# Perceiver block on one core: self-attention in sixteen written-out units with a transposed output, its end interleaved with the output projection

## Chip, cores and metric

The kernel is one program on one core of a Trainium2 chip. The metric is device time in microseconds (us) of one execution, lower is better. The profile is one execution of its own.

## What is computed

Three residual blocks on x of shape (8, 128, 512), cut from the reference:

```python
x = x + cross_attention(layernorm(x), ctx_768, mask, W_q, W_k, W_v, W_o, b_o)   # 8 heads of 64, 8 x 2048 context rows
x = x + self_attention(layernorm(x), Wq, Wkv, Wo)
x = x + ffn(layernorm(x), w_gate, w_up, w_down)                                 # ternary weights, 8-bit activations

def self_attention(h, Wq, Wkv, Wo):          # h: L=8, B=128, 512; 16 heads of 64
    q = (h @ Wq).reshape(L, B, 16, 64)
    k, v = split(h @ Wkv, 2)                 # each (L, B, 16, 64)
    score = einsum('ibnd,jbnd->ijbn', q, k) / 8
    prob = softmax(score, axis=1)            # over j: 8 rows of the same column b
    vec = einsum('ijbn,jbnd->ibnd', prob, v).reshape(L, B, 1024)
    return vec @ Wo
```

The self-attention runs along the first axis of x: each of the 128 columns attends over its own 8 rows. The kernel takes 16 columns times 8 rows as one group of 128 tokens, so there are 8 groups, and one group's scores are a 128 x 128 block of which a constant mask leaves the entries of equal column.

## The kernel before, in words

Every engine has a hand-written instruction list, and semaphores order the engines. All loads and stores are issued by SyncE (SP), in one queue. Weights and activations of most products are split in a high and a low part in a reduced float32 format, and `product` (L536) sums high x high, low x high and high x low, so a product over 512 inputs is 12 matmuls and one over 1024 inputs is 24.

The stages in order of time: query projections; cross-attention, a loop over 8 batches and their live chunks of 256 context rows (13 chunks here); the values of the self-attention for all heads, written to `v_all`; self-attention; output projection together with the transposes of the feed-forward weights; feed-forward.

**Cross-attention, where the change touches it.** `load_chunk` (L316) on SP waits until TensorE has transposed the last context chunk (`cxT_ps`) and until VectorE has turned the last mask row into a bias (`bias_done`), then issues the context load and the mask load. TensorE's `turn_context` (L604) of the next chunk runs after the first scores of the current one. On ScalarE (L989 to L991) the order is two exponentials of the current chunk, then `context_high`, which the next keys (`keys`, L617) wait for.

**Self-attention.** One step of a loop is a pair of heads, `pair(m, first)`, with m from 0 to 7; pair 0 is written out and the loop of pairs 1 to 7 is `Fori(1, PAIRS)`. A pair has two halves of four groups (512 tokens). On TensorE (L816) the order is: query projection and key projection of half 0 (`project`, 12 matmuls each), `finish_pair` of the pair before, query projection of half 1, `scores2` of half 0, key projection of half 1, `turn2` (transposes of the probabilities) for both heads of half 0, `attend2` for both heads, `scores2` of half 1. `attend2` (L800) keeps the transposed probabilities (128 columns) as weights and streams 64 columns of `v_all`, so the result has tokens on the partitions. ScalarE copies queries and one head's transposed probabilities and runs `exp2` (L1088, four exponentials with their sums for each head and half); VectorE copies keys and the other head's probabilities, takes maxima (`top2`, L1549), and in `output2` (L1561) divides by the sums while it copies the result to `o_tok`. The two engines also prepare the weights of the next pair (`weights_high` L1068, `weights_low` L1529, one buffer `wqk`), quantise one eighth of the feed-forward weights per pair (`ternary_clip`, `ternary_round`, `ternary_finish`), and split one eighth of the output weights (`output_weights_high`, `output_weights_low`). GpSimd does nothing in this stage.

**Output projection** (TensorE L837, ScalarE L1140, VectorE L1641, SP L396 to L413). After the last pair, for each of 8 tiles n: ScalarE copies the tile to `o_g`, TensorE transposes it (8 transposes), ScalarE and VectorE split it (`oT`), TensorE transposes tile n of the ternary weights (24 transposes, copied out in three parts), then runs the product of 24 matmuls, and VectorE adds it to `x_all`. `x_all` was stored in `x_mid_dram` and is read back in another token order by eight loads, one per batch, each of which writes 16 partitions (L406). They are issued after the last ternary piece has been stored and the first two have been read back. The feed-forward stage begins when all eight tiles are there (L901).

Of the kernel before, what the change touches and what calls it, by code (L numbers as in the profile page):

```python
# [5 lines left out]
ALU = mybir.AluOpType  # L6
# [8 lines left out]
P = 128  # L15
# [10 lines left out]
def bass_perceiver_block_kernel(nc, x, ctx_768, mask, xa_wq, xa_wk, xa_wv, xa_wo, xa_bo,  # L26
# [30 lines left out]
    with ExitStack() as ctx:  # L57
# [44 lines left out]
        qs = sb("qs", [P, 2, 16])  # L102

# [56 lines left out]
        o_tok = at("o_tok", 88, G, HD2)  # L160
        qT2 = at("qT2", 156, 2, 512)
        kT2 = at("kT2", 160, 2, 512)
        p2 = at("p2", 164, 2, 512)
        pT2 = at("pT2", 168, 2, 512)
        wqk_raw = at("wqk_raw", 8, 2 * DK, P)
        wqk = Split("wqk", 80, 2 * DK, P)
# [4 lines left out]
        tstage = at("tstage", 140, 2, 3 * PIECE, dt=BF16)  # L171
        o_g = at("o_g", 152, 2, HD2)
        oT = Split("oT", 160, 2, HD2)
# [4 lines left out]
        xn_f = at("xn_f", 180, 2, D)  # L178
        xq = at("xq", 76, 2, D, dt=BF16)
        xqT = at("xqT", 78, 2, D, dt=BF16)  # L180
# [13 lines left out]
        def sems(engine, names):  # L194
# [6 lines left out]
         absw_in0, absw_in1, xg_in, wqk_in, wo2_in, traw_in, tern_out, tst_in0, tst_in1, y_out, consts, const_step) = sems(  # L201
            None, "x_in0 x_in1 x_in wq_in wk_in wv_in wo_in bo_in mask_in code_out code_in cx_in mrow_in x_mid_out wv2_in "
            "absw_in0 absw_in1 xg_in wqk_in wo2_in traw_in tern_out tst_in0 tst_in1 y_out consts const_step")
        absw_in, tst_in = [absw_in0, absw_in1], [tst_in0, tst_in1]
        (xnT_ps, q_ps, qT_ps, cxT_ps, kT_ps, s_ps, v_ps, pT_ps, pv_ps, onT_ps, lnT_ps, xo_ps, v2_ps, mean_ps, qk_ps,
         s2_ps, pT2_ps, o2_ps, oT_ps, y2_ps, wT_ps, xqT_ps, g_ps, u_ps, hqT_ps, y_ps) = sems(
            "pe", "xnT_ps q_ps qT_ps cxT_ps kT_ps s_ps v_ps pT_ps pv_ps onT_ps lnT_ps xo_ps v2_ps mean_ps qk_ps "
            "s2_ps pT2_ps o2_ps oT_ps y2_ps wT_ps xqT_ps g_ps u_ps hqT_ps y_ps")
        (wq_hi, wk_hi, wo_hi, xnT_hi, q_done, qT_hi, cxT_hi, kT_hi, v_done, p_done, alpha_done, pT_act, onT_hi, lnT_hi, xo_done,
         wv2_hi, lnTg_done, v2_act, wqk_hi, qT2_done, p2_done, pT2_act, tern_rounded, wo2_hi, og_done, oT_hi, wT_act,  # L210
         xq_done, xqT_done, sg_done, h_round, hq_done, hqT_done, y_scaled) = sems(
            "act", "wq_hi wk_hi wo_hi xnT_hi q_done qT_hi cxT_hi kT_hi v_done p_done alpha_done pT_act onT_hi lnT_hi xo_done "
            "wv2_hi lnTg_done v2_act wqk_hi qT2_done p2_done pT2_act tern_rounded wo2_hi og_done oT_hi wT_act "
# [11 lines left out]
        (rstd_a, wv_hi, w_lo, zeroed, biased, x_mid, rstd_c, rstd_f, scales_done, down_scaled, y_done) = sems(  # L225
            "pool", "rstd_a wv_hi w_lo zeroed biased x_mid rstd_c rstd_f scales_done down_scaled y_done")
# [31 lines left out]
        def live(eng, bits, flag):  # L258

            eng.reg_alu(flag, bits, 1, ALU.bitwise_and)  # L260
            eng.reg_alu(bits, bits, 1, ALU.logical_shift_right)
            return eng.If_ne(flag, 0)

# [33 lines left out]
        def _(sp):  # L297
# [94 lines left out]
            sp.dma_start(tern_dram[PAIRS - 2], tern[:]).then_inc(tern_out, 16)  # L392
            sp.wait_ge(tern_done, START + PAIRS)
            sp.dma_start(tern_dram[PAIRS - 1], tern[:]).then_inc(tern_out, 16)

            sp.wait_ge(o2_ps, START + 4 * PAIRS)  # L396
            sp.wait_ge(tern_out, 16 * PAIRS)

            def load_ternary(piece, u, turned):
                sp.wait_ge(wT_ps, turned)  # L400
                sp.dma_start(tstage[:, u, :], tern_dram[bass.ds(piece, 1)].rearrange("a p n -> p (a n)")).then_inc(tst_in[u], 16)

            for u in range(2):
                load_ternary(u, u, START)
            sp.wait_ge(wo2_lo, START + PAIRS)
            for b in range(B):  # L406
                sp.dma_start(x_all[16 * b:16 * b + 16, :, :],
                             x_mid_dram[b].rearrange("(g q) d -> q g d", q=16)).then_inc(xg_in, 16)
            with sp.Fori(1, G // 2) as t:
                pieces = [sp.snap(2 * t + u) for u in range(2)]  # L410
                turned = sp.snap(START + 6 * t)
                for u in range(2):
                    load_ternary(pieces[u], u, turned)  # L413
# [118 lines left out]
        def _(pe):  # L532
# [237 lines left out]
            def project(m, half, which):  # L770

                if half == 0 and which == 0:
                    pe.wait_ge(wqk_lo, START + m + 1)
# [967 lines left out]
```

## Time and profile before

| | us |
|---|---|
| median of 3 runs | 836.67 (836.04 to 839.28) |
| the profiled execution's own time | 834.46 |
| its span, first to last instruction | 832.5 |

Busy, as a share of the span: TensorE matmul 84% (697.4 us), its weight loads 66%, VectorE 53%, ScalarE 46%, GpSimd 9%. The mean granted TensorE clock is 0.926 of full speed. Read busy time by stage, since each stage has another limit, and read a matmul's own duration with care: matmuls overlap in the pipeline, so the distance from one to the next says more.

### The profile page before, as it was taken

The page shows a single profiled execution, that of the slowest core. Times are in us where ns is not written, and L with a number is a line of the kernel's source. Part 1 is how long each engine was busy: PE and PEld are TensorE (multiplying, and loading weights), DVE is VectorE, ACT ScalarE, POOL GpSimd, SP SyncE. Part 2 cuts the span into 40 slices and gives each one's busy share as a digit, 9 for nine tenths or more (in the row PEclk, how much of TensorE's full clock was granted, in tenths as well). Part 3 has the DMA queues.
Part 4 walks back from the last instruction along what each step waited for, and adds up shares of the span by engine and source line. Part 5 has one row for each costly group of instructions (what it writes and reads, how often), then busy time and mean ns, then how long its engine had stood idle before and what let it go on. Part 6 is the DMA issues. An engine that isn't in the chain of part 4 may idle for free.

```text
span 832.5 us, 15880 instructions
## 1 busy us (share of the span) xinstructions
PE 697.4 (84%) x4310; PEld 551.9 (66%) x4338; DVE 440.3 (53%) x964; ACT 380.0 (46%) x888; POOL 75.5 (9%) x120
## 2 busy tenths in 40 slices
PE   3978579889696969699598999999997499989994
PEld 2767468778585858587386777777776388635452
DVE  6644335534544445446477366665564124699960
ACT  3233324434342444344233466666554235368884
POOL 2480000100101010101100000000000000112211
PEclk9999789979898889799699899999996799999998
DMA  8010000000000000032488224444435912000111
GB/s 291 0 44 0 20 20 20 20 0 20 20 20 20 20 0 20 20 94 115 159 308 289 93 80 144 141 145 138 136 122 173 156 72 79 0 1 14 25 25 38
DMA packets 40133, 64.67 MB, mean 78 GB/s; under 512 B 4138, under 2 KB 20522, under 8 KB 40114
## 3 DMA queue, kind: packets, MB, share of 16 engines
q1 hardware_dynamic: 40114, 64.45, 24.4%
q8 instruction: 8, 0.13, 0.1%
q14 instruction: 11, 0.09, 0.0%
HBM read 53.95 MB, written 10.49 MB: 77 GB/s over the span
## 4 chain that ended last, share of the span: by engine, by line
PE 64%; issue 12%; DVE 8%; ACT 6%; DMA 4%; DVEq 3%; SPq 1%; POOL 1%; ACTq 0%; POOLq 0%
PE bank L545 35%; PE bank L680 6%; PE bank L889 5%; PE bank L806 4%; PE bank L668 3%; PE bank L897 3%; ACT p L1094 3%; DMA x_all<-x_mid_dram 2%; PE bank L653 2%; PE bank L788 2%; PE bank L797 1%; DMA wq_raw<-in_L_xattn_W_q_dram 1%; DVE oT_lo L1276 1%; PE bank L784 1%; DVE amax L1552 1%
## 5 line engine op out<-in xcount | busy, mean ns | idle before, releaser
L979 ACT ACTIVATE probs<-probs,negm 128x256 f32<-128x256 f32 x104 | 52.1, 501 | 105.3 <-DVE negm L1401 105.3
L1401 DVE CUSTOM_DVE_ANT_0 probs<-bank,bias,negm_old 128x256 f32<-128x256 f32 x104 | 46.0, 480 | 60.6 <-PE bank L653 58.4
L1094 ACT ACTIVATE p<-bank,nmax 128x128 f32<-128x128 f32 x128 | 45.0, 378 | 44.4 <-DVE nmax L1554 44.4
L453 POOL TENSOR_TENSOR rstd<-var_eps,neg_half 128x1 f32 (+1 forms) x16 | 10.4, 650 | 592.9 <-DVE var_eps L1623 329.4
L889 PE MATMUL bank<-w_T,xqT 128*128 128x512 bf16 x248 | 57.3, 379 | 4.9 <-ACT xqT L1163 2.0
L653 PE MATMUL bank<-kT_hi,qT_hi 64*128 64x256 f32 x104 | 22.8, 436 | 44.7 <-issue 44.4
L680 PEld LDWEIGHTS bank<-v_sb,pT 128*128 128x128 f32 x416 | 52.3, 191 | 5.5
L680 PE MATMUL bank<-v_sb,pT 128*128 128x64 f32 x416 | 54.7, 274 | 0.0
L972 ACT COPY v_sb<-bank 128x512 f32<-128x512 f32 x28 | 15.1, 590 | 76.5 <-PE bank L680 73.5
L1276 DVE TENSOR_TENSOR kT_lo<-bank,kT_hi 128x512 fp32r<-128x512 f32 x28 | 19.4, 692 | 57.8 <-ACT kT_hi L968 57.8
L653 PEld LDWEIGHTS bank<-kT_hi,qT_hi 64*128 64x128 f32 x104 | 11.1, 210 | 54.0 <-issue 47.0
L889 PEld LDWEIGHTS bank<-w_T,xqT 128*128 128x128 bf16 x256 | 24.1, 98 | 34.2 <-DVE h_f L1670 2.5
L545 PE MATMUL bank<-cxT_hi,wk_hi 128*128 128x256 f32 x168 | 36.4, 328 | 3.2 <-ACT cxT_hi L962 2.7
L545 PE MATMUL bank<-ln_T_hi,wqk_hi 128*128 128x512 f32 x128 | 38.2, 421 | 0.0
L806 PE MATMUL bank<-v_all,pT 128*128 (+1 forms) x256 | 34.1, 288 | 2.9 <-ACT pT L1101 2.9
L1552 DVE TENSOR_REDUCE amax<-bank 128x4 f32<-128x512 f32 x32 | 22.0, 688 | 26.4 <-PE bank L788 26.4
L1524 DVE TENSOR_REDUCE asum<-absw 128x3072 f32 x8 | 26.8, 3354 | 17.2 <-DMA absw<-in_L_ffn_w_down_dram 17.2
L806 PEld LDWEIGHTS bank<-v_all,pT 128*128 128x128 f32 x256 | 32.0, 200 | 5.8 <-issue 4.5
L545 PE MATMUL bank<-ln_T_hi,wqk_lo 128*128 128x512 f32 x128 | 35.3, 398 | 0.0
L545 PE MATMUL bank<-ln_T_lo,wqk_hi 128*128 128x512 f32 x128 | 35.2, 398 | 0.0
L897 PE MATMUL bank<-wd_T,hqT 128*128 128x512 bf16 x124 | 30.3, 396 | 5.1 <-ACT hqT L1187 4.8
L668 PE MATMUL bank<-ident,probs 128*128 128x128 f32 x208 | 33.0, 284 | 0.0
(213 smaller groups left out, 1664.6 us busy)
## 6 DMA issues: line engine op xcount, KB each, us to landing
tern_dram<-tern SPq DMA_DIRECT2D x8, 768.0 KB, 3.6
tstage<-tern_dram SPq DMA_DIRECT2D x8, 768.0 KB, 5.6
cx<-in_ctx_dram SPq DMA_DIRECT2D x14, 384.0 KB, 3.0
absw<-in_L_ffn_w_gate_dram SPq DMA_DIRECT2D x8, 512.0 KB, 3.8
absw<-in_L_ffn_w_up_dram SPq DMA_DIRECT2D x8, 512.0 KB, 4.8
absw<-in_L_ffn_w_down_dram SPq DMA_DIRECT2D x8, 512.0 KB, 6.1
tern_raw<-in_L_ffn_w_gate_dram SPq DMA_DIRECT2D x8, 512.0 KB, 4.6
tern_raw<-in_L_ffn_w_up_dram SPq DMA_DIRECT2D x8, 512.0 KB, 5.8
```

The lines of the kernel that those rows point to most:

```text
L545: last = mm(to, left(k, a), right(k, b), start=(n == 0), stop=(n == 3 * nk - 1))
L653: last = mm(bank[3 + j][:, 0:CHUNK], part(qT, a)[o:o + DH, g, :], part(kT, c)[o:o + DH, g, :], start=(a == c), stop=(a == "lo"))
L668: last = tr(bank[5 + g % 2][:, at:at + P], probs[:, 2 * g + j, t * P:(t + 1) * P], ident[:])
L680: last = mm(bank[7][:, h * DH:(h + 1) * DH], pT[:, g % 2, at:at + P], v_sb[:, t, h * DH:(h + 1) * DH], start=(t == 0), stop=(t == CT - 1))
L806: last = mm(bank[6 + j][:, a * DH:(a + 1) * DH], pT2[:, j, g * P:(g + 1) * P], v_all[:, a, bass.ds(m * P + DH * j, DH)], start=True, stop= ...
L889: last = mm(bank[3 + 2 * which + c % 2][:], xqT[:, u, k * P:(k + 1) * P], w_T[:, which, k, c * 512:c * 512 + 512], start=(k == 0), stop=(k ...
L897: last = mm(bank[7][:], hqT[:, k * P:(k + 1) * P], wd_T[:, k, :], start=(k == 0), stop=(k == FK - 1))
L979: fn(probs[:, h, :], probs[:, h, :], ACT.Exp, bias=negm[:, h:h + 1], scale=-1.0, accum_out=csum[:, h:h + 1]).then_inc(p_done, 1)
L1094: last = fn(p2[:, j, g * P:(g + 1) * P], bank[2 + j][:, g * P:(g + 1) * P], ACT.Exp, bias=nmax2[:, j, g:g + 1], scale=SCALE, accum_out=sum ...
L1276: return tt(to, of, f32(hi), ALU.subtract)
L1401: nc.vector.tensor_tensor_reduce(probs[:, h, :], bank[3 + h % 2][:, 0:CHUNK], bias[:], -SCALE, negm_old[:, h:h + 1], ALU.add, ALU.min, neg ...
L1552: red(amax2[:, j, :], bank[2 + j][:].rearrange("p (g q) -> p g q", q=P), AX_X, ALU.max).then_inc(amax2_done, 1)
```

## The change

- The self-attention loop becomes 16 written-out units u, one per pair and half: m = u // 2, half = u % 2. TensorE's order in a unit is both projections, `attend2(u - 2)`, `scores2(u)`, `turn2(u - 1)`.
- The division by the sums moves to GpSimd and ahead of the transposes: `normalised_p` multiplies a head's probabilities (128 x 512) by the reciprocal sums. `turn2` waits for it. The chain is now exponentials, reciprocal on VectorE (`total2`), multiply on GpSimd, transposes.
- `attend2` keeps 64 columns of `v_all` as weights and streams 128 columns of transposed probabilities; the two heads write partitions 0 to 63 and 64 to 127 of one bank. The result is transposed already and is copied to `o_T`. The copies to `o_g` and the 64 transposes of the output stage go.
- `p2` and the projection weights have two buffers. `weights_high(m + 1)`, `ternary_finish(m)`, `weights_low(m + 1)` and `output_weights_low(m)` stand at the end of the odd unit of pair m.
- The end of the self-attention is interleaved with the first tiles of the output projection; the last product stands behind the transposes of the first feed-forward tile, and the ternary pieces 0 and 1 are read back before the last units are over.
- The residual is read back by eight loads, one per group, each of which writes all 128 partitions. Groups 4 to 7 are read after the last projection, group 0 after the last output weights, groups 1 to 3 after the last ternary piece has been stored.
- The context load is issued without the wait for the bias; the mask load keeps it.

The core of the diff:

```diff
                 sp.wait_ge(cxT_ps, all_turned)
-                sp.wait_ge(bias_done, all_read)
                 sp.dma_start(cx[:], ctx_v[:, ...]).then_inc(cx_in, 16)
+                sp.wait_ge(bias_done, all_read)
                 sp.dma_start(mask_row[:], mask_v[:, ...]).then_inc(mrow_in, 16)
...
+            sp.wait_ge(tern_out, 16 * (PAIRS - 2))
+            load_ternary(0)
+            load_ternary(1)
+            sp.wait_ge(qk_ps, START + 2 * UNITS)
+            for g in range(4, G):
+                gather(g, xg_in1)
+            sp.wait_ge(wo2_lo, START + PAIRS)
+            gather(0, xg_in0)
             sp.wait_ge(tern_done, START + PAIRS)
             sp.dma_start(tern_dram[PAIRS - 1], tern[:]).then_inc(tern_out, 16)
             sp.wait_ge(tern_out, 16 * PAIRS)
+            for g in range(1, 4):
+                gather(g, xg_in0)
...
+            def normalised_p(u, j):
+                pool.wait_ge(rsum2_done, START + 2 * u + j + 1)
+                p = p2[u % 2][j].rearrange("p (g k) -> p g k", k=P)
+                r = of_groups(rsum2, j, u % 2).rearrange("p (g o) -> p g o", o=1).broadcast_to([P, 4, P])
+                nc.gpsimd.tensor_tensor(p, p, r, ALU.mult).then_inc(pn_done, 1)
...
+            def attend2(u):
+                m, half = u // 2, u % 2
+                pe.wait_ge(pT2_act, START + u + 1)
+                pe.wait_ge(pT2_dve, START + u + 1)
+                if u >= 2:
+                    pe.wait_ge(o2_done, START + u - 1)
                 for g in range(4):
+                    for j in range(2):
+                        o = DH * j
+                        last = mm(bank[6 + half][o:o + DH, g * P:(g + 1) * P], v_all[:, 4 * half + g, m * P + o:m * P + o + DH],
+                                  pT2[:, j, g * P:(g + 1) * P], start=True, stop=True)
@@ TensorE @@
+            for u in range(UNITS):
+                project(u, 0)
+                project(u, 1)
+                if u >= 2:
+                    attend2(u - 2)
+                scores2(u)
+                if u:
+                    turn2(u - 1)
...
@@ ScalarE @@
+            for u in range(UNITS):
+                if u >= 2:
+                    prob_copy(u - 2)
+                if u:
+                    exp2(u - 1, 0)
+                query_copy(u)
+                if u:
+                    exp2(u - 1, 1)
+                if half == 0:
+                    ternary_round(m, 0)
+                    ternary_round(m, 1)
                 else:
+                    ternary_round(m, 2)
+                    if m < PAIRS - 1:
                         weights_high(m + 1)
+                    output_weights_high(m)
...
@@ VectorE @@
+            for u in range(UNITS):
+                if u:
+                    top2(u - 1, 0)
+                    top2(u - 1, 1)
+                if u >= 2:
+                    prob_copy2(u - 2)
+                if half == 0:
+                    for w in range(3):
+                        ternary_clip(m, w)
+                if u:
+                    total2(u - 1, 0)
+                key_copy2(u)
+                if u:
+                    total2(u - 1, 1)
+                if u >= 2:
+                    output2(u - 2)
+                if half == 1 and m < PAIRS - 1:
+                    ternary_finish(m)
+                    weights_low(m + 1)
+                    output_weights_low(m)
...
@@ TensorE, after unit 15 @@
+            turn_weights(0, 0)
+            turn_weights(0, 1)
+            attend2(UNITS - 2)
+            turn2_last(0)
             pe.wait_ge(wo2_lo, START + PAIRS)
+            project_out(0)
+            turn2_last(1)
+            project_out(1)
+            attend2(UNITS - 1)
+            turn_weights(0, 2)
+            for n in range(1, G - 1):
+                for w in range(3):
+                    turn_weights(n, w)
+                if n < G - 2:
+                    project_out(n + 1)
+            for w in range(3):
+                turn_weights(G - 1, w)
...
             turn_x(0, 0)
+            project_out(G - 1)
```

After unit 15 ScalarE has `prob_copy(14)`, `exp2(15, 0)`, `out_high(0)`, `exp2(15, 1)`, `out_high(1)`, and VectorE has `top2(15, 0)`, `prob_copy2(14)`, `top2(15, 1)`, `output_weights_low(7)`, `total2(15, 0)`, `output2(14)`, `out_low(0)`, `total2(15, 1)`, `out_low(1)`, `ternary_finish(7)`, `up_copy(0)`, `prob_copy2(15)`, `x2(0)`, `out_low(2)`. `out_high` and `out_low` make the high and low part of one tile of `o_T`; `x2(n)` is the residual add, and `x2(0)` to `x2(3)` wait for all of groups 0 to 3.

## Rows read from the trace of the kernel before

**Rows 1.** The view by stages: busy us of each engine, granted clock, DMA share.

```profile
455.00:628.00 173.00, 162.44 (x1014) 131.36 (x1032) 99.92 (x170) 95.95 (x309) 0.00 (x0) 0.98 0.39 128
628.00:662.00 34.00, 18.70 (x121) 16.05 (x118) 9.21 (x16) 13.87 (x30) 0.00 (x0) 0.69 0.80 163
```

**Rows 2.** The chain that ended last, one pair: start us, us, what.

```profile
511.59 1.14 PE bank L788 x16
...
514.72 1.43 ACT p L1094 x8
...
517.38 1.97 PE bank L806 x16
...
519.78 1.09 PE bank L788 x16
520.88 5.67 PE bank L545 x24
526.55 0.45 PE bank L797 x4
...
533.09 1.14 PE bank L788 x16
```

**Rows 3.** The timeline of the same pair, VectorE and ScalarE: start us, us.

```profile
512.71 0.69 DVE L1552 TENSOR_REDUCE amax<-bank 128x4 f32<-128x512 f32 x1 [1.65 <-PE bank L788]
...
514.52 1.76 DVE L1580 TENSOR_SCALAR tern<-tern_raw 128x3072 bf16 x1
...
518.13 1.23 DVE L1276 TENSOR_TENSOR wqk_lo<-wqk_raw,wqk_hi 128x1024 fp32r<-128x1024 f32 x1
...
528.16 2.25 DVE L1575 TENSOR_SCALAR tern_raw<-tern_raw,wmean,nmean  x3
...
529.15 3.23 ACT L1108 ACTIVATE tern_raw<-tern_raw,wscale  x3 [1.47 <-DVE tern_raw L1575]
```

**Rows 4.** GpSimd's 128 x 512 additions, line 485: ns min/median/max.

```profile
L485 POOL TENSOR_TENSOR x_all<-x_all,bo x8: 1281/1290/1720, 51.5 to 60.8; 128x512 f32<-128x512 f32 x8
```

**Rows 5.** The timeline where GpSimd and VectorE work on SBUF together.

```profile
51.70 1.73 DVE L1276 TENSOR_TENSOR qT_lo<-qT_all,qT_hi 128x512 fp32r<-128x512 f32 x1
...
395.47 1.24 POOL L453 TENSOR_TENSOR rstd<-var_eps,neg_half 128x1 f32 x1 [3.88 <-DVE var_eps L1464]
```

**Rows 6.** The waits, cross-attention: us in total, times, longest us.

```profile
PE bank L610 <- DMA cx<-in_ctx_dram: 4.9, 5, 1.1
```

**Rows 7.** The timeline behind one such wait.

```profile
240.87 0.49 ACT L979 ACTIVATE probs<-probs,negm 128x256 f32<-128x256 f32 x1
...
241.36 0.56 ACT L962 CAST cxT_hi<-bank 128x512 fp32r<-128x512 f32 x1
...
241.97 0.66 PE L545 MATMUL bank<-cxT_hi,wk_hi 128*128 128x256 f32 x3 [0.28 <-ACT cxT_hi L962]
```

**Rows 8.** The chain from the last scores to the feed-forward stage.

```profile
627.36 1.14 PE bank L788 x16
...
641.83 18.97 DMA x_all<-x_mid_dram
...
663.04 8.00 PE bank L545 x24
...
673.47 5.75 PE bank L545 x24
...
722.41 6.87 PE bank L889 x31
```

**Rows 9.** The timeline of one tile's weight transposes.

```profile
671.75 1.50 PE L856 MATMUL bank<-ident_b,tstage 128*128 128x128 bf16 x24
```

**Rows 10.** DMA issues: KB each, median us to landing.

```profile
tern_dram<-tern SPq DMA_DIRECT2D x8, 768.0 KB, 3.6
...
wo_raw<-in_L_attn_Wo_dram SPq DMA_DIRECT2D x8, 256.0 KB, 2.6
x_all<-x_mid_dram SPq DMA_DIRECT2D x8, 256.0 KB, 13.7
```

More of the change, by code:

```diff
@@ L102, in bass_perceiver_block_kernel @@
         qs = sb("qs", [P, 2, 16])
+        p2_odd1 = sb("p2_odd1", [P, 512])
         BASE = 25600
@@ new lines, in down_copy @@
+            def down_copy(n):
+                act.wait_ge(wT_ps, START + 3 * n + 3)
+                cp(wd_T[:, 2 * n:2 * n + 2, :].rearrange("p j c -> p (j c)"), bank_b[4 if n == 0 else 6]).then_inc(wT_act, 1)
+            prob_copy(UNITS - 2)
+            exp2(UNITS - 1, 0)
+            out_high(0)
+            exp2(UNITS - 1, 1)
+            out_high(1)
+            gate_copy(0)
+            prob_copy(UNITS - 1)
+            out_high(2)
+            down_copy(0)
+            for n in range(1, G - 1):
+                if n < G - 2:
+                    out_high(n + 2)
+                gate_copy(n)
+                down_copy(n)
@@ L1530, in weights_low @@
                 dve.wait_ge(wqk_hi, START + m + 1)
-                low(wqk.lo[:], wqk_raw[:], wqk.hi[:]).then_inc(wqk_lo, 1)
+                low(wqk_lo_of[m % 2][:], wqk_raw[:], wqk_hi_of[m % 2][:]).then_inc(wqk_lo, 1)
             weights_low(0)
@@ L1587, in pair @@
-            def pair(m, first):
-                key_copy2(m, 0)
-                if not first:
-                    prob_copy2(m - 1, 1)
-                ternary_clip(m)
-                if not first:
-                    output2(m - 1)
-                    output_weights_low(m - 1)
-                top2(m, 0, 0)
-                top2(m, 0, 1)
-                if not first:
-                    ternary_finish(m - 1)
-                key_copy2(m, 1)
-                prob_copy2(m, 0)
-                if isinstance(m, int):
-                    weights_low(m + 1)
-                else:
-                    with dve.If(m < PAIRS - 1):
-                        weights_low(m + 1)
-                top2(m, 1, 0)
-                top2(m, 1, 1)
@@ L1609, in _ @@
-            dve.wait_ge(v2_dve, START + G)
-            pair(0, True)
-            with dve.Fori(1, PAIRS) as m:
-                pair(m, False)
-            ternary_finish(PAIRS - 1)
-            prob_copy2(PAIRS - 1, 1)
-            output2(PAIRS - 1)
-            output_weights_low(PAIRS - 1)
+                low(wo2.lo[:, m, :], wo2_raw[:], wo2.hi[:, m, :]).then_inc(wo2_lo, 1)
+            dve.wait_ge(v2_dve, START + G)
+            for u in range(UNITS):
+                m, half = u // 2, u % 2
+                if u:
+                    top2(u - 1, 0)
+                    top2(u - 1, 1)
+                if u >= 2:
+                    prob_copy2(u - 2)
+                if half == 0:
+                    for w in range(3):
+                        ternary_clip(m, w)
+                if u:
+                    total2(u - 1, 0)
+                key_copy2(u)
+                if u:
+                    total2(u - 1, 1)
+                if u >= 2:
+                    output2(u - 2)
+                if half == 1 and m < PAIRS - 1:
+                    ternary_finish(m)
+                    weights_low(m + 1)
+                    output_weights_low(m)
@@ new lines, in _ @@
+            top2(UNITS - 1, 0)
+            prob_copy2(UNITS - 2)
+            top2(UNITS - 1, 1)
+            output_weights_low(PAIRS - 1)
+            total2(UNITS - 1, 0)
+            output2(UNITS - 2)
+            out_low(0)
+            total2(UNITS - 1, 1)
+            out_low(1)
+            ternary_finish(PAIRS - 1)
+            up_copy(0)
+            prob_copy2(UNITS - 1)
+            x2(0)
+            out_low(2)
+            output2(UNITS - 1)
+            for n in range(1, G - 1):
+                x2(n)
+                if n < G - 2:
+                    out_low(n + 2)
+                up_copy(n)
+                if n == G - 3:
+                    dve.wait_ge(x2_done, START + 1)
+                    ln_a(0, 0)
+                    ln_b(0, 0)
+                    ln_c(0, 0)
```

364 lines of the change are left out of this document (157 added, 207 removed).

## Prediction

> **What bounds the kernel now.** I read the busy times by stage first, then the chain that ended last inside the stages that the diff touches, then the timeline of one pair for the durations on the other engines, last the waits and the DMA rows. By stage, TensorE is busy for 162.4 of 173 us in the self-attention at a clock of 0.98, but only for 18.7 of 34 us behind it, at 0.69 [rows 1]. The second window is where time lies idle. The chain of one pair is nearly all TensorE: projections, scores, transposes and values follow each other, and a pair takes 533.09 - 511.59 = 21.5 us [rows 2]. So the self-attention is bound by TensorE's work plus short waits. The chain behind the last scores begins to leave them at 627.36 + 1.14 = 628.5 and reaches the feed-forward stage at 722.41 [rows 8]: 93.9 us, of which 18.97 are one wait for the residual's read from DRAM.
>
> **Context load without the bias wait: nothing.** TensorE waits for the context load five times, 4.9 us in all [rows 6]. Behind such a wait the next keys start at 241.97 when ScalarE's cast is done; the cast started at 241.36 right behind an exponential that began at 240.87 and lasted 0.49 [rows 7]. ScalarE would come to that cast no sooner if the transposes were ready earlier, so the wait lies beside the exponentials. The sum takes 0. Ends: 0 and the whole 4.9 us. The load writes a buffer that `cxT_ps` still guards, and the mask load behind it in SP's queue waits for the bias as before, so nothing gets later.
>
> **One pair of units.** TensorE's terms: two projections are 24 matmuls, 5.67; scores from the end of the values before (517.38 + 1.97 = 519.35) to 520.88, 1.53; four transposes 0.45, so 0.9 a unit; values 1.97 a half [rows 2]. The old pair is 2 x (5.67 + 1.53 + 0.9 + 1.97) = 20.1, and 1.4 of waits make 21.5.
>
> The new values product streams 128 columns in 16 instructions, with weights half as wide, and its two heads take different halves of the array's columns. No row shows that form. The nearest is the scores product, also 16 instructions of 128 columns with its two heads in different halves (of the rows): 1.09 to 1.14 [rows 2]. If the heads did not overlap, 16 instructions would cost as the transposes do, 0.45 / 4 = 0.11 each, 1.8, and the old 1.97 I take as the upper end. I take 1.3, near the scores, with something for the change of shape on both sides. TensorE's work is then 2 x (5.67 + 1.53 + 0.9 + 1.3) = 18.8 a pair.
>
> The even unit takes that, 9.4: the old waits go, since a unit's transposes now stand behind the next unit's projections. The multiply must still be in time. Count from the end of unit u - 1's scores (then its predecessor's transposes, 0.9, follow). First head: maximum 0.8 (0.69 and a short instruction; a copy of 512 columns I take as 0.6 to 0.7 after the same row) [rows 3], exponentials 1.4 (half of eight in about 2.9; 1.43 is the chain's piece), ended near 2.6. ScalarE then waits for the query projection of unit u, which ends at 0.9 + 2.84 = 3.75, copies it (0.6) and does the second head's exponentials: 5.8. VectorE takes the reciprocal behind the key copy, which ends at 0.9 + 5.67 + 0.8 = 7.4; at 7.6 GpSimd starts the second multiply, 1.29 [rows 4], and ends at 9.0. TensorE wants it at 0.9 + 5.67 + 1.3 + 1.53 + 0.45 = 9.85. Hidden, with 0.85 to spare. If that cover is gone the excess is paid per unit: a multiply of 1.72, the longest of those rows, uses up half of it, and a second stretch on the same engine the rest.
>
> The odd unit is longer. Behind the key projection VectorE has the key copy and the reciprocal, then `output2`, which waits for the values: 1.3 + 0.1 + 0.7. Then come `ternary_finish` 1.76 and `weights_low` 1.23 [rows 3], and the next projections wait for the latter. GpSimd's second multiply runs beside the start of `ternary_finish`; I charge 0.3. Sum 2.1 + 0.3 + 1.76 + 1.23 + 0.1 = 5.5 against TensorE's own 1.3 + 1.53 + 0.9 = 3.7. So TensorE stands 1.7 us once a pair, a new wait for `wqk_lo`. `ternary_round` (3.23 for three) and the casts fit on ScalarE [rows 3]. The pair: 9.4 + 5.67 + 5.5 = 20.5. Eight pairs by 1.0: 8 us gained. Queued behind the late `weights_low` are `output_weights_low` and the next maxima (0.69 each), 2 to 3 us late; the same pair's slack on TensorE, two projections, holds them.
>
> The two SBUF clients disturb each other: a 512-column VectorE subtraction took 1.73 beside GpSimd's additions while one of 1024 columns takes 1.23, and a one-column GpSimd instruction took 1.24 beside such a subtraction [rows 3, 5]. The Trainium skill ("GPSIMD Engine Reference", Specifications) says that the SBUF interfaces are shared, with contention for VectorE instructions with two SBUF inputs or in a two-port mode. By that rule all of the clips, `ternary_finish` and the subtractions would collide; by the rows I count one collision a pair. This is rival 3.
>
> **From the last scores to the feed-forward stage.** Counted from the end of unit 15's scores. The first product needs `attend2(14)`, `output2`, ScalarE's cast of 1024 columns and VectorE's subtraction: transposes 0.9; the probability copy ends at 1.8; values to 3.2; copy to 4.0; cast to 5.2; subtraction (1.23) to 6.6. Product 0 runs to 12.3, four transposes, product 1 to 18.4 (5.67 each, as 24 matmuls above; rows 8 show 5.75 in this stage). Values of unit 15 and the rest of tile 0's transposes to 20.2. The next transposes wait for a copy of 1.0: 21.3, and are done at 22.8, since a tile's 24 take 1.5 [rows 9]. Products 2 to 6 and the four sets of transposes between them: 5 x 5.67 + 4 x 1.42 = 34, to 56.8. Two sets of transposes and one more copy wait: 4.2; the first feed-forward tile 0.4; product 7 5.67: 67.1. The last add 0.8: 68. Against 93.9 that is 26 us. They are: the wait of 18.97 (what is late next is product 0, 6.6 us after the scores); eight transposes a tile with their copies; the half clock, at which the product behind the wait took 8.00 instead of 5.75 [rows 8].
>
> The reads of the residual must be in time. Group 0 to 3 need the last ternary piece stored: `ternary_finish(7)` ends at about 10.8, its store 3.6 later [rows 10], 14.5. Three reads that write 128 partitions are like the loads of the output weights, 2.6 us for the same 256 KB; the old ones had 13.7 [rows 10]. With three issues they land at 18.5 to 19, the add and the next subtraction end at 21, and product 2 starts at 22.8: hidden by 1.8. At 13.7 they would not be.
>
> I leave out a fall of the clock where TensorE idles 1.3 to 1.7 us twice ahead of product 0; before, it was at half rate after an idle 2.5 us. Price, if it falls: up to 8.00 - 5.75 = 2.3. I put 1 us for it.
>
> **Sum.** 8 + 26 - 1 = 33. The profiled execution took 834.46 (span 832.5), so about 801 for one of the same kind; the median of the runs is 836.67, 2.2 above it, so I forecast 836.67 - 33, about 803.
>
> **Rivals.**
> 1. The heads do not overlap in the new product, 1.97: the even unit loses 0.7, the odd one 0.7 by `output2`, 1.4 a pair, 11 us: 814. For it: no row shows column halves. Against: the row halves overlap. The Trainium skill ("TensorEngine Tiling (Array Packing)", Key Properties) says that a change of tiling mode drains the engine; here two more changes a unit, which would push towards this case. The trace shows no price of them apart from the 1.53 that the scores take with theirs.
> 2. The residual's reads keep 13.7: landing at 28.2, product 2 at 30.2 instead of 22.8: 7.4 us, 810. For it: the same source, 1.5 MB of other traffic near it. Against: 128 partitions, three reads instead of eight.
> 3. GpSimd and VectorE hold each other up: multiplies of 1.72 and a second collision, 0.6 a pair, 5 us: 808.
> 4. The context wait counts fully: 4.9 less, 798.
> 5. Slower than before: the multiply with its broadcast operand. Two a unit stand in series; above about 1.6 us each they outlast TensorE's cover and each further microsecond costs about 1.25 us a unit, 20 in all. From 1.6 + 33 / 20 = 3.3 us a multiply the gain is gone; at 4.0 the time is 803 + 48 = 851. Against: plain ones take 1.29.
>
> **How the numbers follow.** Forecast 50%, rival 1 17%, rival 2 10%, rival 3 14%, rival 4 6%, rival 5 3%. The low end takes rival 4 (798) with values at 1.14, 0.3 a pair: 795. The high end takes rival 1 with part of 3: 817. About 0.5%, 4 us, is what a measurement of this kernel tells from no change. Faster 0.96, same 0.01, slower 0.03.
>
> **What would show it.** After: about 20.5 us from one even unit's projections to the next; a TensorE wait for `wqk_lo` of 1 to 2 us once a pair; values product near 1.3; multiplies at 1.3 to 1.7; no wait of TensorE for the context and yet the same distance to the keys; about 68 us from the last scores to the first feed-forward matmul, with the clock near full; residual reads near 3 us. Wrong if transposes wait for the multiply in every unit, or if an add waits for the residual longer than 2 us.

## The result, and the profile after

The changed kernel takes 799.07 us (median of 4 runs, 795.08 to 801.29) against 836.71 (836.04 to 839.28): a ratio of 0.9545, 95% interval 0.9515 to 0.9576. A second series gave 797.98 and 0.9541 (0.9516 to 0.9565). The forecast was about 803.

The profiled execution took 799.53 with a span of 797.6. The view by stages, columns as in [rows 1], self-attention and the 34 us behind its last scores:

```profile
462.00:618.00 156.00, 147.20 (x1010) 113.51 (x1011) 99.55 (x183) 96.23 (x309) 32.68 (x30) 0.99 0.45 152
618.00:652.00 34.00, 30.11 (x202) 24.67 (x203) 16.74 (x23) 14.49 (x29) 2.08 (x2) 0.90 0.40 137
```

Against [rows 1], TensorE is busy for 30.1 us of the 34 instead of 18.7, and the self-attention is 156 us long instead of 171. GpSimd has appeared, with 33 us of work. The chain that ended last, one pair (start us, us, what), answers to [rows 2]:

```profile
511.61 5.47 PE bank L571 x24
517.08 1.05 PE bank L841 x16
...
518.19 0.57 issue
518.76 1.86 DVE tern L1630
520.63 1.14 DVE wqk_odd_lo L1327
...
521.82 5.74 PE bank L571 x24
527.56 1.02 PE bank L841 x16
528.58 0.54 PE bank L814 x2
529.12 1.09 PE bank L818 x16
530.21 1.02 PE bank L829 x8
531.23 1.84 PE bank L571 x8
```

From one odd unit's projections (511.61) to the next (531.23) is 19.62 us. The odd unit takes 10.21 and leaves TensorE for VectorE: it runs through the values' copy, `ternary_finish` and the low weights. The even unit (521.82 to 531.23) is TensorE's alone, 9.41. The waits of TensorE (us in total, times, longest):

```profile
PE bank L571 <- DVE wqk_odd_lo L1327: 3.6, 4, 1.1
PE bank L571 <- DVE wqk_even_lo L1327: 3.2, 3, 1.1
PE bank L873 <- ACT wd_T L1188: 2.4, 2, 1.2
PE bank L859 <- POOL p_odd L513: 1.5, 1, 1.5
PE bank L571 <- DVE oT_lo L1327: 1.2, 1, 1.2
```

GpSimd's multiplies by groups (busy us, mean ns of one; idle before them). Most take 1.04 us; one, in the first pair, took 2.46:

```profile
L513 POOL TENSOR_TENSOR p_even<-p_even,rsum 128x512 f32<-128x512 f32 x16 | 18.1, 1131 | 119.8 <-DVE rsum L1609 119.8
L513 POOL TENSOR_TENSOR p_odd<-p_odd,rsum 128x512 f32<-128x512 f32 x16 | 16.7, 1042 | 63.5 <-DVE rsum L1609 63.4
```

The chain behind the last scores answers to [rows 8]:

```profile
616.86 1.09 PE bank L818 x16
...
624.25 8.49 PE bank L571 x24
...
633.18 5.49 PE bank L571 x24
640.28 1.02 ACT wd_T L1188
...
642.94 5.53 PE bank L571 x24
...
680.34 5.54 PE bank L571 x24
685.88 1.01 issue
686.88 3.18 PE bank L923 x14
```

The last scores end at 616.86 + 1.09 = 617.95; the feed-forward stage begins at 686.88, 68.9 us later, where it was 93.9. Product 0 took 8.49 us, product 1 5.49.

VectorE waited for the residual's read, in front of the add for tile 0:

```profile
638.88 0.69 DVE L1694 TENSOR_TENSOR x_all<-x_all,bank 128x512 f32<-128x512 f32 x1 [4.97 <-DMA x_all<-x_mid_dram]
```

By stage, the profile of before has the first projections of the self-attention at 457.1, the end of the last scores at 628.5, the first feed-forward matmul at 722.4 and the end of the span at 832.5. The profile of after has 462.0, 617.95, 686.9 and 797.6. So the self-attention gained 15.4 us, the part behind it 25.0, the feed-forward stage lost 0.6; and the part in front, where only the context wait is different, was 4.9 longer. Together 34.9.

### The profile page after: what moved, and what is told of

Read it like the earlier page. It is cut to its first block, busy times and chain, and to the rows that moved or that the text cites. A ratio compares the mean times of both kernels' runs of the same rounds, so it can differ in the third digit from the quotient of the medians.

```text
span 797.6 us, 15089 instructions
## 1 busy us (share of the span) xinstructions
PE 674.9 (85%) x4274; PEld 526.5 (66%) x4274; DVE 442.4 (55%) x972; ACT 372.3 (47%) x872; POOL 109.7 (14%) x152
## 4 chain that ended last, share of the span: by engine, by line
PE 70%; issue 11%; DVE 10%; ACT 3%; DVEq 3%; POOL 1%; DMA 1%; ACTq 0%; SPq 0%; POOLq 0%
PE bank L571 41%; PE bank L706 6%; PE bank L923 5%; PE bank L694 3%; PE bank L931 3%; PE bank L679 2%; PE bank L841 2%; DVE tern L1630 2%; PE bank L818 1%; PE bank L873 1%; DMA wq_raw<-in_L_xattn_W_q_dram 1%; PE bank L829 1%; DVE wqk_odd_lo L1327 1%; ACT cxT_hi L999 1%; DVE h_f L1735 1%
## 5 line engine op out<-in xcount | busy, mean ns | idle before, releaser
L571 PE MATMUL bank<-cxT_hi,wk_hi 128*128 128x256 f32 x168 | 38.0, 340 | 4.0 <-ACT cxT_hi L999 3.6
L513 POOL TENSOR_TENSOR p_even<-p_even,rsum 128x512 f32<-128x512 f32 x16 | 18.1, 1131 | 119.8 <-DVE rsum L1609 119.8
L571 PE MATMUL bank<-cxT_lo,wk_hi 128*128 128x256 f32 x168 | 31.9, 302 | 1.7 <-DVE cxT_lo L1327 1.7
L1599 DVE COPY kT<-bank 128x512 f32<-128x512 f32 x16 | 11.1, 692 | 38.9 <-PE bank L571 38.9
L571 PEld LDWEIGHTS bank<-cxT_hi,wk_hi 128*128 128x128 f32 x168 | 27.0, 215 | 7.5 <-ACT cxT_hi L999 6.8
L571 PE MATMUL bank<-cxT_hi,wk_lo 128*128 128x256 f32 x168 | 31.9, 303 | 0.0
L1133 ACT ACTIVATE p_odd<-bank,nmax 128x128 f32<-128x128 f32 x64 | 22.7, 371 | 15.7 <-DVE nmax L1605 15.7
L571 PEld LDWEIGHTS bank<-cxT_lo,wk_hi 128*128 128x128 f32 x168 | 27.0, 210 | 2.0 <-DVE cxT_lo L1327 1.9
```

The source lines that it names most:

```text
L513: nc.gpsimd.tensor_tensor(p, p, r, ALU.mult).then_inc(pn_done, 1)
L571: last = mm(to, left(k, a), right(k, b), start=(n == 0), stop=(n == 3 * nk - 1))
L1133: last = fn(p2[u % 2][j][:, g * P:(g + 1) * P], bank[2 + j][:, g * P:(g + 1) * P], ACT.Exp, bias=nmax2[:, j, g:g + 1], scale=SCALE, accum_ ...
```

## Experiments

Times are medians; a ratio is to the kernel before, run on the same chip in turn. "Changed kernel" is the one forecast.

**The context load.** Two kernels, one with this edit alone, one with all the others:

```
 # ctx_only: kernel before; ctx_old: changed kernel with the reverse
-sp.wait_ge(bias_done, all_read)
 sp.dma_start(cx[:], ...)
+sp.wait_ge(bias_done, all_read)
```

> The kernel before, with one edit: the context load is issued without the wait for the bias; all else as before. Theory A (the prediction's): the next keys wait for ScalarE's cast, which stands behind the exponentials, so the load's earlier landing changes nothing: ratio 1.000, within 0.3%. Theory B (the waits count): the five waits of 4.9 us are gained, 0.994. Theory C (drift seen in the profile of after, where the self-attention starts 5 us later than before): the earlier load costs something at the passages between batches: 1.003 to 1.006. The chain decides: the start of the self-attention's first projections is 457.2 in the profile of before.

> The changed kernel with the old order of the two waits: context load behind the wait for the bias. Theory A: same time as the changed kernel, 799 within 2.5 us. Theory B: 4.9 us slower than it, 804. Theory C: 3 to 5 us faster than it, 795, and the self-attention starts near 457 instead of 462.

Alone it gave 838.69, ratio 0.9998 (0.9976 to 1.002). Taken back it gave 796.95, 0.9516 (0.9489 to 0.9543), whose interval overlaps that of the changed kernel. TensorE's wait of 4.9 us for the load [rows 6] is in neither the profile of the edit alone nor that of the changed kernel. It did not vanish but moved to two waits behind it: for VectorE's maxima, 0.3 us in the profile of before, and for ScalarE's cast, 2.2 before. In the profile of the edit alone they are

```profile
PE bank L653 <- DVE negm L1401: 4.1, 6, 0.8
PE bank L545 <- ACT cxT_hi L962: 3.0, 6, 0.6
```

Together they grew by 4.6 us. At the passage of [rows 7] the distance from the first scores to the next keys is 3.37 us in both profiles (238.60 to 241.97, and 243.35 to 246.72), and in both it is the cast that releases the keys. Theory A holds to 0.3%: the wait went and brought nothing. Theory C fails. The self-attention began at 463.4 in the profile of the edit alone, but that kernel's median is that of the kernel before, and over all 14 profiles of this study it began between 457.1 and 463.4, with the early load at 458.8 to 463.4 and with the late one at 457.1 and 460.1. The 4.9 us are a spread between executions. It goes with the granted clock: from 50 to 150 us the clock was 0.90 in the two profiles that reached the self-attention first (457.1, 458.8) and 0.83 in the three that reached it last (463.0 to 463.4), but also in one at 460.7. What sets the clock there stays open.

**VectorE's order.**

```
 if half == 1 and m < PAIRS - 1:
-    ternary_finish(m)
     weights_low(m + 1)
+    ternary_finish(m)
     output_weights_low(m)
```

> The changed kernel with one exchange in VectorE's order: in odd units the next pair's low weights are made before the pair's ternary weights are finished. Theory A: TensorE's wait once a pair for those weights (1.06 to 1.29 us in the profile of after, seven times) is caused by the 1.86 us of the ternary instruction in front of them; it goes, 7 to 8 us faster than the changed kernel: 791 to 792. Theory B: the weights wait for the values' copy and ScalarE's cast anyway, or the ternary instruction only delays the key copy or the maxima behind it instead: 0 to 2 us faster, 797 to 799.

788.05, ratio 0.9403 (0.9378 to 0.9427): 10 to 11 us faster than the changed kernel. Its chain, from one set of values to the next but one:

```profile
503.76 1.02 PE bank L841 x16
504.79 0.46 issue
...
507.74 5.47 PE bank L571 x24
513.21 1.02 PE bank L841 x16
514.24 0.16 issue
...
516.89 5.47 PE bank L571 x24
522.36 1.02 PE bank L841 x16
```

The pair is 18.60 us, all TensorE but for 0.6; the wait for the low weights is in no row. From the first projections to the last maxima it takes 150.4 us instead of 157.6, which is Theory A's 7. Theory B fails. The rest of the 10 to 11 us is not the pair. Against the first profile of the changed kernel it is 2.4 us of the clock in the tail (below) and 1.3 of an earlier start of the self-attention; against its second, in which the clock did not fall, it is 2.3 of that start alone. So 7 us are shown for the exchange, and the other 3 to 4 are not shown to be its work.

**The multiply's cover.**

```
-nc.gpsimd.tensor_tensor(p, p, r, ALU.mult).then_inc(pn_done, 1)
+nc.gpsimd.tensor_tensor(p, p, r, ALU.mult).then_inc(pn_half, 1)
+pool.wait_ge(pn_half, START + 2 * u + j + 1)
+one_p = ...    # a column of ones, broadcast to [P, 4, P]
+nc.gpsimd.tensor_tensor(p, p, one_p, ALU.mult).then_inc(pn_done, 1)
```

> The changed kernel with a second GpSimd instruction of 512 columns behind each multiply (by ones, in place), so that each result is ready about 1.1 to 1.2 us later; the computation is the same. Theory A (the multiply is hidden with about 0.65 us to spare before the transposes, as the profile of after shows): only the excess is paid, about 0.5 us for each of 16 units, 6 to 12 us: 805 to 811. Theory B (the multiply is on the path already): 1.1 to 2.3 us a unit, 18 to 37 us: 817 to 836. Theory C (wide cover): below 3 us: 799 to 802. Side effect to look for: VectorE's two-input instructions that run beside GpSimd get longer.

812.0, ratio 0.9686 (0.9656 to 0.9716): 13 us slower than the changed kernel, a little above the range of A and below that of B. So the multiply was hidden, and the cover is short. TensorE's waits in the self-attention are 18.5 us in this profile and 8.8 in that of after, 9.7 more, which is inside the range of A. Groups of GpSimd and VectorE (busy us, mean ns):

```profile
L516 POOL TENSOR_TENSOR p_even<-p_even,ones 128x512 f32<-128x512 f32 x14 | 23.8, 1699 | 1.1
L516 POOL TENSOR_TENSOR p_odd<-p_odd,ones 128x512 f32<-128x512 f32 x14 | 14.6, 1040 | 1.1
L1330 DVE TENSOR_TENSOR wqk_odd_lo<-wqk_raw,wqk_odd_hi 128x1024 fp32r<-128x1024 f32 x4 | 8.2, 2058 | 0.0
```

The second multiplies of the even probabilities now meet `ternary_finish` and the low weights. The multiply takes 1.04 us elsewhere and 2.43 there, the subtraction for the low weights 2.06 instead of 1.21. The timeline shows in which way:

```profile
521.64 1.86 DVE L1633 TENSOR_SCALAR tern<-tern_raw 128x3072 bf16<-128x3072 f32 x1
521.97 2.43 POOL L516 TENSOR_TENSOR p_even<-p_even,ones 128x512 f32<-128x512 f32 x1
523.42 2.06 DVE L1330 TENSOR_TENSOR wqk_odd_lo<-wqk_raw,wqk_odd_hi 128x1024 fp32r<-128x1024 f32 x1
```

The multiply starts while `ternary_finish` runs and ends at 524.40, 0.9 us behind its end, nearly a whole multiply. The low weights start at 523.42 and end at 525.48, 1.1 us behind the multiply's end, nearly a whole subtraction. So the figures look like one engine holding the other up until it is done, not like two that run side by side at a slower pace.

The collision is only a part of the surplus. Three times in this self-attention the granted clock also fell, which it did in no profile of the changed kernel behind the stage's first projections: the 24 matmuls behind a wait took 6.95, 7.37 and 7.35 us instead of 5.7, 4.4 us in all. With the 9.7 us of waits that is 14.1 of the 14.6 us by which the stage is longer in this profile.

**The values product.**

```
-for g in range(4):
-    for j in range(2):
+for j in range(2):
+    for g in range(4):
```

> The changed kernel with the loops of the values product exchanged: the four groups of the first head, then the four of the second, so that instructions that follow each other write the same half of the columns. The computation is the same. Theory A (the 1.02 to 1.09 us for 16 instructions come from two heads running beside each other in different column halves; apart they would cost as the transposes do, 0.11 each, 1.8): the product takes 1.7 to 2.0, and with 0.7 to 0.9 more in each unit, in odd ones by the values' copy on VectorE, 12 to 14 us: 810 to 813. Theory B (the instructions are as short without a partner): 1.0 to 1.1 us as now, 799 within 2.5.

803.7, ratio 0.9599 (0.9561 to 0.9637), 5 us slower than the changed kernel. Its chain has for the product

```profile
519.48 1.52 PE bank L841 x16
```

where the changed kernel has 1.05. The two kernels differ in the order alone, so the order is what the product gains from, and that fits A's neighbours in different column halves running beside each other; but apart they cost 1.51 to 1.52, not the 1.7 to 2.0 that I had expected. The loss is 0.5 a unit. The self-attention is 5.9 us longer, not 16 x 0.5: only 14 of the products stand in it, and TensorE's waits for the low weights shrank from 6.8 to 6.0, because `ternary_finish` takes 1.75 there instead of 1.86. Even without the overlap the new form would have beaten the old 1.97 [rows 2].

**The residual's reads.**

```
-for g in range(4, G): gather(g, xg_in1)      # behind the last projection
-gather(0, xg_in0)
 # behind the last ternary store:
-for g in range(1, 4): gather(g, xg_in0)
+for b in range(B): sp.dma_start(x_all[16 * b:16 * b + 16, :, :], ...)
```

> The changed kernel with the residual's reads as in the kernel before: eight reads of 16 partitions each, all issued behind the last store of ternary weights. The ternary loads keep their early place. Theory A (the prediction's rival 2: the reads' form and place decide when product 2 can run): issues from 631.6 on, eight of 0.6 to 0.7 us, the last landing 5 to 14 us later, 637 + 5 = 642 to 650, against 638.9 now; the add and the subtraction behind it 1.9, so product 2 starts 3 to 9 us later than 642.9: 802 to 808. Theory B (the 18.97 us wait of the kernel before belongs to the reads whatever stands beside them): it comes back minus the two products that now run over it, 631.6 + 19 = 651, 8 to 10 us later than now: 808 to 811.

810.39, ratio 0.9694 (0.966 to 0.9728): 11 to 12 us slower. The DMA issues of this stretch (KB, median us to landing):

```profile
x_all<-x_mid_dram SPq DMA_DIRECT2D x8, 256.0 KB, 9.9
```

The waits of VectorE and of TensorE, and then the timeline at product 2:

```profile
DVE x_all L1691 <- DMA x_all<-x_mid_dram: 17.6, 1, 17.6
...
PE bank L568 <- DVE oT_lo L1324: 11.8, 2, 10.5
```

```profile
649.21 3.78 PE L568 MATMUL bank<-wo_hi,oT_hi 128*128 128x512 f32 x8 [10.53 <-DVE oT_lo L1324]
```

The last read lands at 647.33, 15.2 us behind its issue. The scores end 2.8 us earlier in this profile than in that of after; counted from there, product 2 is 9.1 us late, and at the slow clock behind the wait it takes 8.3 instead of 5.5. That is 11.9, the price in the profile. It lies above A (3 to 9) and at or a little above B (8 to 10, without the clock): the wait does not come back whole, but most of it.

The edit changes two things at once, the form of the reads and their place, so it does not say what either is worth. The view by windows, this kernel while nothing but its reads is under way, then the changed kernel while its last three do (the last two numbers are the busy share of the DMA engines and GB/s), shows that the form counts:

```profile
632.50:636.00 3.50, 3.49 (x33) 2.56 (x31) 0.00 (x0) 0.00 (x0) 0.00 (x0) 1.00 1.08 119
633.60:638.90 5.30, 5.30 (x29) 4.13 (x29) 0.33 (x2) 0.28 (x1) 0.00 (x0) 1.00 0.39 140
```

At a rate no higher the reads of 16 partitions keep the DMA engines fully busy, those of 128 for two fifths of the time. Eight late reads of 128 partitions were not run.

**The waits in the tail.** Two edits on top of the order of VectorE:

```
 # two_edits, turn_weights(n, w)
-START + (n if w == 1 else 2 * n)
+START + (2 * n - 1, n, 2 * n)[w]
 # three_edits, x2(n)
-dve.wait_ge(xg_in0 if n < 4 else xg_in1, 16 * 4)
+n == 0: dve.wait_ge(xg_first, 16)    # the read of tile 0 has its own
```

> The version with the low weights before the ternary instruction (788.05), and in the tail TensorE's transposes of the gate weights wait only for the copy of the bank that they write, no longer for ScalarE's copy of the down weights too. In the profile of the changed kernel TensorE waits twice for that copy, 2.4 us in all. Theory A: both waits go or shrink to under 0.3 us: 786. Theory B: the copy of the down weights is needed for the third set of the same piece anyway, and only moves there: 787.5 to 788.

> The version with two edits (788.38), and the residual's read for tile 0 has a semaphore of its own, so that the add for tile 0 no longer waits for the reads of tiles 1 to 3. In the profile of that version product 2 waits 1.4 us for a subtraction that stands behind this add, and the add waits 7.6 us for the reads, until 629.98. Theory A: the reads behind the last ternary store have become what sets product 2; the 1.4 us go: 787. Theory B: the copy of the down weights and the cast behind it on ScalarE (629.66 to 630.7) set it as well: only 0.1 to 0.3 us, 788.2.

788.38 (0.9425, 0.9397 to 0.9453) and 787.32 (0.9413, 0.9383 to 0.9444). The first removed its waits, 2.4 us down to 0.5 (0.2 for this copy, 0.3 for another), and the time stayed. TensorE's waits, and the add for tile 0 in the timeline:

```profile
PE bank L571 <- DVE oT_lo L1327: 2.6, 2, 1.4
...
PE bank L873 <- ACT wd_T L1188: 0.2, 1, 0.2
```

```profile
629.98 0.69 DVE L1694 TENSOR_TENSOR x_all<-x_all,bank 128x512 f32<-128x512 f32 x1 [7.56 <-DMA x_all<-x_mid_dram]
```

Where the copy had been late, the residual's reads now are. I had named the copy itself as what would remain; that was wrong. The second edit took that 1.4 us away too (1.2 left, which is product 0's), and 1.1 us of the median, too little to tell by itself.

**Two places for the last wait of a pair.** Both on top of the three edits:

```
 # turn_split: transposes of the first head ahead of the scores
+turn2(u - 1, 0)
 scores2(u)
-turn2(u - 1)
+turn2(u - 1, 1)
...
 # clip_moved: ternary_clip(m, 2) behind output2(u - 2)
```

> The version with three edits, and in the self-attention the transposes of the first head stand before the scores of the next unit instead of behind them, the second head's stay behind. Theory A: TensorE waits 0.46 us in one unit and 0.16 in the next for the keys' copy between the values and the scores; four transposes (0.5 us) cover it, 0.6 us a pair, 4 to 5 us less than with three edits: 782. Theory B: in units with three clips in front of the reciprocal, the first head's multiply ends at the time at which the scores start now, and the transposes only take the wait over: 0 to 1.5 us less: 786.

> The version with three edits, and the third clip of the ternary weights stands behind the values' copy on VectorE instead of in front of the first reciprocal and the keys' copy. Theory A: the keys' copy comes 0.8 us earlier in every second unit and TensorE's wait of 0.46 us there goes: 3 to 4 us less than with three edits: 783.5. Theory B: the clip then delays the first maxima of the next unit's softmax by as much, and the exponentials and the multiply behind it: 0 or slower, 787 to 789.

790.79 (0.947, 0.9438 to 0.9502) and 784.78 (0.9391, 0.9359 to 0.9422). TensorE's waits, first the one, then the other:

```profile
PE bank L829 <- POOL p_odd L513: 5.5, 7, 1.1
```

```profile
PE bank L814 <- issue: 3.0, 15, 0.8
```

Splitting the transposes was slower, which neither theory had: in one unit of two the first head's multiply is not done yet, and TensorE waits 0.8 us in seven units, 5.5 in all. The wait that was to go fell from 5.7 us to 0.4, and yet the self-attention is 4.4 us longer: the pair is 19.14 us instead of 18.59. Behind the new wait the transposes take 0.66 + 0.59 us in two parts where eight in one take 1.02; what is left of the difference stays open. Moving the clip made the pair 18.29 us instead of 18.59 and that wait 3.0 us instead of 5.7. The medians differ by 2.5 us, as 8 x 0.30 = 2.4 says, though their intervals overlap. This last version is the fastest of the study, 13 to 14 us below the changed kernel.

**The clock behind the last scores.** The changed kernel once more, and a variant of it:

```
 attend2(UNITS - 2)
+pe.wait_ge(p2_done, START + 2 * UNITS - 1)
+pe.wait_ge(wo2_lo, START + 1)
+fill(5)     # matmuls of 512 columns that nobody reads
 turn2_last(0)
+fill(4)
```

> The changed kernel, unchanged, once more: for a narrower interval of its time and to see which readings of its profile repeat. Theory A: the start of the self-attention (462 in its first profile, 457 to 463 in the others with either order of the context waits) moves by some us from run to run; the fall of the clock between the last scores and product 0, which stands in all five profiles of kernels with the old order of VectorE (changed kernel and four variants of it) and in none of the five with the new one, comes again: granted clock near 0.5 for 4 to 6 us from 6 us behind the last scores. Time 799 within 2. Theory B: the fall is chance, clock 1.00.

> The changed kernel with nine matmuls of 512 columns whose results nobody reads, five in front of the last unit's first transposes and four in front of product 0, where TensorE stands 1.46 and 1.23 us. They write a bank that product 0 starts anew. Theory A (the clock falls because TensorE idles there, and that costs what product 0 takes above 5.6 us, 8.49 - 5.6 = 2.9, less what the fillers overrun): clock 1.00 behind the scores, 796 to 797. Theory B (the fall comes from the 1.1 us waits once a pair before it, or from chance): product 0 stays at 8 us or so, and the time at 799 to 800.

797.98, and 795.83 (0.9522, 0.9496 to 0.9549). The view by windows, first the first profile of the changed kernel, then its second; the third number from the end is the granted clock:

```profile
621.00:624.00 3.00, 0.66 (x4) 0.42 (x4) 1.89 (x4) 2.20 (x8) 1.04 (x1) 0.90 0.52 191
624.00:630.00 6.00, 5.75 (x14) 4.52 (x15) 4.00 (x5) 2.59 (x5) 1.04 (x1) 0.50 0.21 82
```

```profile
622.00:625.00 3.00, 0.66 (x4) 0.42 (x4) 1.81 (x3) 2.38 (x10) 1.04 (x1) 1.00 0.52 188
625.00:631.00 6.00, 5.93 (x29) 4.96 (x29) 3.89 (x4) 2.55 (x5) 1.04 (x1) 1.00 0.22 90
```

One kernel, the same idle times of 1.46 and 1.23 us, and the clock goes to half (1.2 of 2.4 GHz) once and not the other time. From the start of product 0 to the transposes behind it are 8.33 us and 5.54. Theory A of the repeat fails in that point. Over all profiles: with the old order of VectorE the clock fell in five of six, with the new one in none of five, and not with the fillers. The fillers' profile has 64.9 us from the last maxima to the feed-forward stage, the second profile of the changed kernel 65.0, the first 67.3; so they gain nothing over an execution in which the clock does not fall, and the median's 2 us are within the intervals. That the waits once a pair make the fall likely is what the counts suggest; it is not shown.

## Why the prediction was right, and where it was off

**Context load.** Right: nothing, by the cover named; the distance to the keys is the same 3.37 us.

**The pair.** The mechanism was right, its gain half the size: 8 us forecast, 15.4 measured. The even unit is 9.41 against 9.4. The mis-sized term is the odd unit, 5.67 + 5.5 = 11.2 against 10.21. Its parts: projections 5.47; values 1.05 where I had 1.3; values' copy and the gap 0.6 where I had 0.8; `ternary_finish` 1.86, of which 0.1 is GpSimd (it takes 1.75 where no multiply runs), where I had charged 1.76 + 0.3; low weights 1.14 on the chain for 1.23. Each was rounded up on the one chain that decides, and eight times 0.96 is 7.7. TensorE's new wait is 6.8 us for seven pairs, 1.0 each, not 1.7. And `wlow_first` shows that the wait was not needed at all.

**Values product.** 1.02 to 1.05 where I had 1.3; the lower bound, the scores' row, was the better guide than the middle.

**Multiply.** 1.04 to 1.13 on average instead of 1.29, hidden: TensorE waited for it 0.3 us outside the tail, behind the one multiply of 2.46. The spare time was as short as forecast; a doubled one costs 13 us.

**Tail.** 68.9 us against 68 + 1; 66.6 in the second profile (618.8 to 685.4). Product 0 starts 6.3 us behind the scores (6.6 forecast), product 2 at 25.0, and at 22.4 without the fall of the clock (22.8). The residual's reads were hidden by less than I said: they landed 20.9 and 20.5 us behind the scores, not 18.5 to 19, and in the second profile TensorE did wait 0.27 for what stands behind them. The mis-sized term is the landing: the first of the last three reads was issued 13.7 us behind the scores, earlier than the 14.5 forecast, but the third landed 5.3 us behind the end of its issue where I had taken 2.6. My own sign of being wrong, an add that waits for the residual longer than 2 us, came true: the add for tile 0 waited 4.97 us, and 7.4 in the second profile. The sign was badly chosen, since products 0 and 1 ran meanwhile and what counts is TensorE's wait. I had priced a fall of the clock at up to 2.3 and taken 1; it is 2.8 on product 0 and 2.3 on the stage.

**The sum.** 33 forecast, 38 measured. The stages say 15.4 + 25.0 to 27.3 - 0.6, 40 to 42, and the difference to the medians is inside the spread of the part in front. That 803 came within 0.5% of the time is luck in part: the pairs gave 7.4 us more than forecast, and in the profile 5.5 of that were lost again in the part in front and in the feed-forward stage, on which the forecast has nothing.

**Rivals.** 1 (heads do not overlap, 814): false, and its price was too high, 803.7. 2 (slow reads, 810): false for this form and place. The old form and place gave 810.4, near its 810 by luck: the delay is 9.1 us where the rival had 7.4, 2.8 of the clock come on top, and both count from 799, not 803. 3 (GpSimd and VectorE hold each other up): all but absent here, though the mechanism is real. The multiplies mostly meet copies out of the matmul banks, or begin a little ahead of `ternary_finish` and cost it 0.1 us. In the first pair alone one met it as in the doubled kernel: the multiply took 2.46 us and the low weights 2.06. The Trainium skill ("GPSIMD Engine Reference", Specifications) names contention with VectorE instructions that have two SBUF inputs or run in a two-port mode. The runs agree for the subtraction of two inputs, 1.21 us alone and 2.06 behind a multiply. `ternary_finish`, with one tensor input, was held up as well, 2.59 instead of 1.75 once in the doubled kernel; no run shows in which mode it ran. 4 (context): false. 5 (slow broadcast multiply): false, 1.04 us; the broadcast operand costs nothing that shows.

## What to carry to other kernels

Once transposes and softmax are a unit apart, what decides is the order on the engine that feeds the next weights: a short result that TensorE waits for belongs ahead of a long one that nobody waits for, and that exchange was worth 7 us of the stage here. A removed wait is only worth the distance to what is late next, so read that row first (the context load: nothing; the copy of the down weights: nothing, until the reads behind it were split). Eight reads of 16 partitions, all issued behind the last store, made TensorE's next product 9 us late and cost 3 more by the clock; the same bytes in reads of 128 partitions, five of eight issued ahead of that store, cost at most 0.3 us. How much of this is the form and how much the place was not measured. And when a variant costs more than its waits, look at the granted clock before blaming a mechanism.

## What the runs showed of the hardware that I had not expected

- 16 fp32 matmuls with weights of 64 columns and 128 streamed columns took 1.02 us when neighbours wrote different column halves, and 1.51 when they wrote the same half. The gain of the order is a third, not a half.
- GpSimd's multiply of 128 x 512 with an operand broadcast along 128 elements took 1.04 us; the additions of [rows 4] with plain operands 1.29. The operation differs too, so the broadcast is not shown to be the cause.
- GpSimd's multiply and VectorE's instructions on SBUF held each other up, as if in turns: a multiply that began while `ternary_finish` ran took 2.43 us instead of 1.04, and the subtraction of two inputs that began behind it 2.06 instead of 1.21.
- Reads of 16 partitions kept the DMA engines fully busy at 119 GB/s, reads of 128 partitions for two fifths at 140 GB/s.
- The granted clock fell to half in one execution of a kernel and stayed full in another, behind the same idle times.
